# GpSimd's scatters of the last batch tied to VectorE's gating in the expert stages

## What is computed

```python
probs = softmax(x @ gate_weight.T)
top_vals, top_idx = top_k(probs, 8)          # 32 experts
# the smallest prefix with a share of 0.8 is kept (at most 7 here), renormalised
for each expert e:
    g, u = split(x @ w_gu[e].T)
    out += (silu(g) * u) @ w_d[e].T * combine[:, e]
```

## Time and profile before

| | |
|---|---|
| median of 3 runs | 1107.92 us (1105.23 to 1110.94) |
| span of the profiled execution, first to last instruction | 1109.5 us |
| expert stage f | about 288 to 524 us |
| softmax attention | about 524 to 831 us |
| expert stage g, with its reads and adds | about 831 to 1109 us |
| PE busy | 882.3 us (80%) |
| POOL busy | 647.3 us (58%) |
| DVE busy | 583.1 us (53%) |
| ACT busy | 549.3 us (50%) |

### The profile page before, as it was taken

One profiled execution on the slowest core, in us unless ns is written; L12 is line 12 of the kernel. 1 busy time (PEld: TensorE's weight loads), 2 busy tenths in 40 slices (PEclk: granted clock), 3 DMA queues, 4 the chain that ended last, 5 costly groups with the idle time before them and its releaser, 6 DMA issues. The chain is left out here.

```text
span 1109.5 us, 20646 instructions
## 1 busy us (share of the span) xinstructions
PE 882.3 (80%) x5504; PEld 667.1 (60%) x5504; DVE 583.1 (53%) x2104; ACT 549.3 (50%) x1088; POOL 647.3 (58%) x636
## 2 busy tenths in 40 slices
PE   5999998861588899997388987988658889999930
PEld 3666666541478799996243543534227778999830
DVE  4566785875364222226776587764623622222665
ACT  6333455730254455654267775775515454555520
POOL 2465658777666677776720011364655567777773
PEclk9999999995699999999679998988888999999975
DMA  9900002122649886783430011135327588767875
GB/s 343 381 4 2 1 25 84 72 84 82 196 163 306 285 263 219 221 268 131 144 133 34 34 34 44 44 113 212 112 104 238 188 282 276 233 217 249 288 244 195
DMA packets 93231, 181.64 MB, mean 164 GB/s; under 512 B 18985, under 2 KB 73788, under 8 KB 92736
## 3 DMA queue, kind: packets, MB, share of 16 engines
q1 hardware_dynamic: 68544, 114.19, 31.7%
q0 software_dynamic: 24576, 66.13, 16.3%
HBM read 96.34 MB, written 92.27 MB: 170 GB/s over the span
## 5 line engine op out<-in xcount | busy, mean ns | idle before, releaser
L1295 POOL DMA_INDIRECT result_rows<-ys,result_slots x288 | 291.5, 1012 | 104.1 <-issue 93.7
L981 POOL DMA_INDIRECT expert_rows<-route_rows,index x224 | 223.5, 998 | 99.8 <-issue 90.3
L1946 ACT ACTIVATE b_probs<-ps 128x1024 f32<-128x1024 f32 x128 | 127.8, 1031 | 43.9 <-PE ps L1795 43.3
L1447 PE MATMUL ps<-w_gu,g_xts 128*128 x576 | 109.1, 333 | 3.0 <-ACT g_xts L1490 2.2
L1447 PE MATMUL ps<-w_gu,f_xts 128*128 x576 | 108.6, 333 | 2.4 <-ACT f_xts L1490 1.9
L1447 PEld LDWEIGHTS ps<-w_gu,g_xts 128*128 128x128 f32 x576 | 94.6, 195 | 5.1 <-issue 4.9
L1447 PEld LDWEIGHTS ps<-w_gu,f_xts 128*128 128x128 f32 x576 | 94.5, 194 | 3.7 <-issue 3.6
L1540 DVE SCALAR_TENSOR_TENSOR f_h<-ps,f_xs,f_gate 128x96 f32<-128x96 f32 x144 | 39.2, 313 | 100.0 <-ACT f_gate L1497 98.5
L1540 DVE SCALAR_TENSOR_TENSOR g_h<-ps,g_xs,g_gate 128x96 f32<-128x96 f32 x144 | 39.0, 313 | 96.8 <-ACT g_gate L1497 89.6
L1807 PE MATMUL ps<-b_probs,b_v_pad 128*32 128x512 f32 x512 | 78.2, 686 | 11.4 <-issue 5.6
L1508 ACT COPY ys<-ps 128x512 f32<-128x512 f32 x144 | 83.6, 581 | 2.0 <-PE ps L1466 2.0
(11 more groups left out here) (362 smaller groups left out, 1827.6 us busy)
## 6 DMA issues: line engine op xcount, KB each, us to landing
parts<-result_rows SPq DMA_DIRECT2D x32, 896.0 KB, 5.2
f_xs<-expert_rows SPq DMA_DIRECT2D x144, 160.0 KB
g_xs<-expert_rows SPq DMA_DIRECT2D x144, 160.0 KB
expert_rows<-pad_rows SPq DMA_DIRECT2D x64, 160.0 KB
w_gu<-in_Wgu SPq DMA_DIRECT2D x1, 6144.0 KB, 17.6
expert_rows<-pad_rows SPq DMA_DIRECT2D x1, 5120.0 KB, 39.7
result_rows<-ys,result_slots POOLq DMA_INDIRECT x288, 3.3
f_w_d<-in_Wdown SPq DMA_DIRECT2D x1, 4096.0 KB, 29.4
```

What stands on the lines that cost most here:

```text
L981: self.nc.gpsimd.indirect_dma_start(xs, bass.IndirectOffsetOnAxis(self.index[:, f, t, r:r + 1].bitcast(U32), 0), self.x_rows(f)[:, t, :], ...
L1295: self.nc.gpsimd.indirect_dma_start(self.y_dram, bass.IndirectOffsetOnAxis(self.slots[:, i, j:j + 1].bitcast(U32), 0), self.ys[:, i, j, :] ...
L1447: ins = nc.tensor.matmul(ps[:, bank_gu[u % 2], j * GU:(j + 1) * GU], xts[:, u % 2, o:o + P], w_gu[:, k, bass.ds(experts[j] * GU, GU)], sta ...
L1946: nc.scalar.activation(probs[:, u % RING, :, :], ps[:, 2 * (u % 2):2 * (u % 2) + 2, :], ACT.Exp, scale=float(HD) ** -0.5).then_inc(exp_don ...
```

## The change

In the GpSimd program of both expert stages each x scatter of the last batch (`B - 1`, that is 3) gets a wait ahead of it. In slot u it waits until `h_ready` has reached u - 1, which is the end of the gating of slot u - 2. The order of GpSimd's instructions, the data and all other engines' programs stay as they are.

```diff
@@ -1556,6 +1556,8 @@
                 for step, f in steps_at(u):
                     routing.gpsimd(pool, step, f)
                 for f, k in scatters_at(u):
+                    if f == B - 1:
+                        pool.wait_ge(h_ready, u - 1)
                     routing.scatter(pool, f, k, xs_dram)
                 for v in results_at(u):
                     pool.wait_ge(y_ready, v + 1)
```

## The result

| | before | after |
|---|---|---|
| median | 1106.58 us (4 runs, 1104.50 to 1110.94) | 1119.88 us (4 runs, 1114.89 to 1121.45) |
| ratio after to before | | 1.0106, 95% interval 1.0069 to 1.0143 |
| span of the profiled execution | 1109.5 us | 1118.2 us |
| its device time | | 1119.99 us |

The change makes the kernel about 12 us slower. By medians it is 13.3 us, by the ratio 11.7 us, and its interval reaches from 7.6 to 15.8 us. With the same 1.8 us the profiled execution of before took about 1111.3 us, an estimate; that is longer than each of its runs in the table, and so the two spans alone show only 8.7 us of difference.

A forecast was written before the change was run, and what follows sets the result against it. POOL's unbroken run of result scatters was taken to set the ends of both expert stages. 8.1 us in stage f plus 3.6 us in stage g gave 11.7 us, so 1107.9 + 11.7 = 1119.6 us, range 1113 to 1125.

The forecast's parts named there:

- What bounds: Ends of both expert stages: POOL's backlog of result scatters decides; about 2.9 us of stage f's end are POOL's alone.
- Nothing hides it: End of stage f: ACT and DVE have no share, so the full 8.1 us delay is paid.
- The term of stage f: Stage f: result scatters start at 377.7 instead of 369.60, costing 8.1 us.
- Where POOL stands still: x scatters: POOL pauses 3 to 4 us after 14 and 28, for everything issued on the oldest one's semaphore.
- R: Start of POOL's long run of result scatters: 377.7 instead of 369.60 in stage f, 915.0 instead of 911.00 in g.
- Stage g: Stage g: result scatters start 4.0 us later, of which the end keeps 3.6 us.
- What else waits: SP's slot 26 load hides behind the pads; reuse of the result ring is covered; the attention only begins 8.1 us later.
- The rival of a feedback through late loads: Stage f: spread x scatters delay SP's loads, gating 21 and the end by 5 us; 1124.6 us, chance 0.08.
- No pauses: x scatters: pauses come from scatter rate and go when spread; 4 us slower in all, 1111.9 us, chance 0.08.
- Faster by room for the loads: Slots 22 to 25: spread scatters leave loads room, PE loses less; at most 9 us gained, 1099 us, chance 0.04.
- no effect: New waits do nothing because DVE is ahead; 1108 us, chance 0.03.
- Cheap landings: Pauses at x scatters: spread scatters land in 2.2 us; 8.1 us slower in all, 1116.0 us, chance 0.15.

The follow-up runs named there:

- e2_g_only: Kernel before with the new waits in stage g only; 1111.36 us, ratio 1.0026 (1.0003 to 1.0050).
- e5_split_before: Kernel before with the x scatters of batch 3 on four semaphores, one per token tile, instead of one; 1106.14 us, ratio 0.9997.
- e1_f_only: Kernel before with the new waits in stage f only; 1113.06 us, ratio 1.0047 (1.0028 to 1.0066).
- e4_fill: Changed kernel, waits kept, with three result pairs in stage f and two in g moved into the waiting time; 1106.36 us, ratio 0.9986 to before.
- e9_after_again: The changed kernel run once more, unaltered (the second set of runs); 1118.61 us, ratio 1.0084 to the kernel before.
- e6_split_after: Changed kernel with the x scatters of batch 3 on four semaphores instead of one; 1110.54 us, ratio 1.0042 to the kernel before.
- e8_best: Kernel before with four semaphores and two result pairs of stage g already in slot 8; 1103.13 us, ratio 0.9977.
- e10_best_again: The same kernel as e8_best, run once more; 1105.86 us, ratio 0.9980 to the kernel before.
- e11_sums_earlier: Kernel of e8_best with the sums of stage g begun two slots earlier; 1101.43 us, ratio 0.9937 to the kernel before.

## Why the prediction was right, and where it was not

- **What bounds.** Right for the end of stage g: there POOL decides. For stage f right in the profiled execution, but called too firmly. The prediction put POOL's lead at 2.9 us, from ACT's last copy to the start of the next stage. The barrier itself takes 1.33 us behind ACT's last copy (e2_g_only, and as much in e5_split_before), so the lead was 1.5 us, and in another execution of the same code it was 2.6 us the other way; over the profiles PE's side is as a rule a little later. "Nothing hides it" is wrong for stage f. The term of stage f, 8.1 us, is right as a shift of POOL and too large as a loss on average: 5.2 us (3.1 to 7.3) in e1_f_only, 6.3 us between the profiles.
- **Where POOL stands still.** Right for this kernel, and now shown: same scatters, same distance of 14, gone with a semaphore for each tile, and the pauses of before end behind the last packet of GpSimd's queue. Too wide in one point: it is not everything on the oldest one's semaphore that is waited for, but the unbroken row on it, as e4_fill shows. In the kernels before and after the rows are unbroken, so the sum isn't touched.
- **Stage f.** R was put 8.1 us later. From PE's first matmul of the stage it is 86.48 us instead of 78.44: 8.0 us (8.8 in e9_after_again). The parts were less exact than their sum, and two errors cancel. The pauses are 2.84 and 2.76 us instead of the 3.78 and 3.40 taken. And a scatter starts 0.8 to 1.0 us behind the end of the gating that it waits for (slot 12: 340.30 to 341.31, slot 23: 372.77 to 373.58), where 0.1 was taken. The gates themselves came about 1 us later, with the stage.
- **Stage g.** R was put 4.0 us later and is 6.3 us later (83.4 against 77.0 us). The term that was mis-sized is the pauses, 4.48 and 4.01 us against 3.38 and 3.52, which is 1.6 of the 2.3 us. They are landings under load, and a landing under load scatters: 2.8 to 5.1 us over the profiles here. The other 0.7 us is again the step from gate to scatter, 0.81 us at slot 12 (gating 10 ended at 884.51) where 0.1 was taken. In e9_after_again R is 5.3 us later. Of the 6.3 us 0.6 went in the run of result scatters, and at the end 1.0 us was given back rather than 0.4, since the two last reads now go out 0.85 us apart instead of 1.50 and their adds stand one behind the other. POOL's last scatter is 9.7 us later than 1091.79 and not 12, mainly because the attention was 4.5 us shorter in this execution.
- **What else waits.** Right: SP's load of slot 26 still goes out behind the pads, at 381.63 instead of 381.36 (timelines of SP and PE after):

```profile
381.63 1.25 SPq L1390 DMA_DIRECT2D f_xs<-expert_rows  x2
...
383.87 1.07 PE L1435 MATMUL ps<-ident,f_xs 128*128 128x128 f32 x4 [2.09 <-DMA f_xs<-expert_rows]
```

  PE waited 2.09 us for the load of slot 25 here, where it waited 0.72 us before, and ended the stage 3.3 us later, 0.9 of it from the later start of the stage. The rival of a feedback through late loads exists in this size and doesn't decide, because POOL ends later still.
- **The size.** 11.7 us forecast, 11.7 us in the first set of runs (7.6 to 15.8) and 9.3 us in the second. That the first agrees to a tenth is luck: its interval is 8 us wide, stage f costs less than was put down, and what stage g costs is open: 3.6 us were put down, the profiles give 6.2, the time of e2_g_only 2.9 us (0.3 to 5.5).
- **The rivals.** "No pauses" falls with e5_split_before and its time (4 us) came out in e6_split_after, where the pauses are really taken away. "Faster by room for the loads" and "no effect" fall with the result. Cheap landings (2.2 us as in the attention) didn't come. The estimate of 1.4 us for a pause, worked out from the fit of the Trainium skill ("DMA: Bandwidth & Descriptors", section "Anatomy of one DMA — SWDGE (gpsimd) path"), is missed by every pause measured in the expert stages. In the attention the last packet moves 2.2 us behind the issue at 745.60, near the 2.4 us of that estimate for the whole DMA, and GpSimd goes on 1.0 us later; in stage f it moves 3.4 us behind the issue at 343.87.

## What to carry to other kernels

An engine that is busy 58% of the span can still set the end, if it works through a backlog without a gap up to the last instruction: look for the group whose idle time before each instruction is the bare issue gap. A wait put in front of such a backlog is paid where that engine is last, less what the others need anyway, and costs nothing if other work of the same engine fills it, as e4_fill did with the waits left in. Before a loss is put down to one of two engines that end within 2 us of each other, look at a second execution of the same code.

## What the runs showed of the hardware

- GpSimd issues these indirect DMAs of 128 rows every 1.28 us. Behind 14 in a row on one semaphore it stands until its queue has no packet left, and goes on 0.9 to 1.4 us later: 2.8 to 5.1 us of idle time in the expert stages, 2.2 us in the attention (once 2.9). With four semaphores of 7 scatters each the pauses are gone in all profiles (e5_split_before, e6_split_after, e8_best, e10_best_again, e11_sums_earlier). Other DMAs in between break the row: in e4_fill, where result scatters with semaphores of their own stand between the first x scatters, the only pauses at the x scatters of batch 3 are 4.08 us in stage f and 3.27 us in stage g, each behind 14 in a row. All kernels here are built with `dynamic_dma_scratch_size=2048` (line 2361 of the kernel before). No run changes it, so whether the 14 is a matter of the chip or of this setting is open.
- In stage g of before the result scatters that overlap one of DVE's adds on `parts` or `X` take 1.16 us on average (30 of them, 12 over 1.05 us), the 108 others 0.97 us, and none of these is over 1.05 us.
- The untouched attention took between 301.8 and 310.5 us in the profiles of this study, the longest two at a granted clock of 0.85, the shortest at 0.90. That scatter is as large as many an edit, and two single profiles can't tell an effect of that size.
